# A gated recurrence on one core: Candidate's low-part product widened to 128 columns, so that it carries both parts of its input

## What is computed

```
z = sigmoid(xz_t + h @ U_z + vz)
r = sigmoid(xr_t + h @ U_r + vr)
hh = tanh(xh_t + (r * h) @ U + vh)
h = (1 - z) * h + z * hh          # for t = 0 .. 127
x = x + all h
```

## Time and profile before

| | |
|---|---|
| runs before | 1509.14 us median of 3 (1508.98 to 1510.17) |
| profiled execution | 1510.37 us, span 1508.5 us, mean TensorE clock 0.998 |
| TensorE busy | 1499.4 us, 99% |
| VectorE, ScalarE busy | 84%, 78% |
| the recurrence | from 551 us to the end |

### The profile page before, as it was taken

One profiled execution on the slowest core, in us unless ns is written; L12 is line 12 of the kernel. 1 busy time (PEld: TensorE's weight loads), 2 busy tenths in 40 slices (PEclk: granted clock), 3 DMA queues, 4 the chain that ended last, 5 costly groups with the idle time before them and its releaser, 6 DMA issues.

```text
span 1508.5 us, 54085 instructions
## 1 busy us (share of the span) xinstructions
PE 1499.4 (99%) x22906; PEld 1175.1 (78%) x22906; DVE 1260.1 (84%) x2548; ACT 1173.7 (78%) x2726; POOL 315.7 (21%) x332
## 2 busy tenths in 40 slices
PE   9999999999999999999999999999999999999998
PEld 6874444444444467779999999999999999999998
DVE  7999999999999887777878787778787887776677
ACT  7989999999999835667777777777777777777444
POOL 1100111111110014322222222222222222222222
PEclk9999999999999999999999999999999999999999
DMA  5155365565638978533333333333333333320000
GB/s 199 33 159 183 96 200 140 130 159 136 191 84 133 142 115 102 74 52 23 48 20 48 48 20 49 43 25 48 20 46 48 20 48 20 48 41 3 31 32 31
DMA packets 545106, 116.61 MB, mean 77 GB/s; under 512 B 520160, under 2 KB 527200, under 8 KB 536160
## 3 DMA queue, kind: packets, MB, share of 16 engines
q1 hardware_dynamic: 537424, 82.14, 31.4%
q0 software_dynamic: 7008, 30.41, 10.7%
q10 hardware_dynamic: 432, 0.59, 0.1%
HBM read 66.47 MB, written 33.55 MB: 66 GB/s over the span
## 4 chain that ended last, share of the span: by engine, by line
PE 99%; DMA 0%; DVE 0%; ACT 0%; issue 0%; DVEq 0%
PE ps L1552 33%; PE ps L1617 22%; PE ps L1654 20%; PE ps L1666 15%; PE ps L1638 6%; PE ps L1570 2%; DMA AR<-in_w1f 0%; PE ps L1519 0%; PE ps L1583 0%; DVE ST L1381 0%; ACT ST L942 0%; ACT W L619 0%; DVE RL L1438 0%; ACT XS L626 0%; DVE ST L1386 0%
## 5 line engine op out<-in xcount | busy, mean ns | idle before, releaser
L1552 PE MATMUL ps<-XH,WH 128*128 128x512 f16 x1872 | 404.7, 379 | 0.0
L1552 PEld LDWEIGHTS ps<-XH,WH 128*128 128x128 f16 x1872 | 182.9, 98 | 220.2 <-issue 0.3
L1654 PE MATMUL ps<-HL,U 128*128 128x64 f16 x6112 | 221.0, 193 | 1.9 <-DVE HL L1485 1.9
L1773 POOL TENSOR_TENSOR ST<-ST 128x256 f32<-128x256 f32 x126 | 114.5, 909 | 490.9 <-ACT ST L934 490.9
L1666 PE MATMUL ps<-HL,U 128*128 128x64 f16 x4064 | 214.3, 206 | 0.0
L1654 PEld LDWEIGHTS ps<-HL,U 128*128 128x128 f16 x6112 | 204.8, 98 | 8.0 <-issue 2.0
L1666 PEld LDWEIGHTS ps<-HL,U 128*128 128x128 f16 x4064 | 183.5, 98 | 0.0
L1654 PEld LDWEIGHTS ps<-RL,U 128*128 128x128 f16 x4064 | 135.1, 98 | 6.5 <-issue 1.2
L1654 PE MATMUL ps<-RL,U 128*128 128x64 f16 x4064 | 139.4, 193 | 0.3 <-issue 0.3
L902 ACT ACTIVATE ST<-ps,dn 128x128 f32<-128x128 f32 x252 | 78.4, 361 | 71.2 <-PE ps L1666 71.1
L949 ACT ACTIVATE HL<-ST 128x128 f16<-128x128 f32 x208 | 53.3, 302 | 80.3 <-DVE ST L1477 80.3
(11 more groups left out here) (213 smaller groups left out, 3113.0 us busy)
## 6 DMA issues: line engine op xcount, KB each, us to landing
x_scratch<-AR SPq DMA_DIRECT2D x16, 1024.0 KB, 5.3
AR<-in_x POOLq DMA_DIRECT2D x15, 1024.0 KB, 7.9
AR<-HB POOLq DMA_DIRECT2D x11, 1024.0 KB, 7.0
raw<-x_scratch SPq DMA_DIRECT2D x88, 128.0 KB, 4.2
out_y<-raw SPq DMA_DIRECT2D x11, 1024.0 KB, 4.0
raw<-in_x SPq DMA_DIRECT2D x10, 1024.0 KB, 7.3
ST<-in_x SPq DMA_DIRECT2D x5, 1024.0 KB, 7.4
out_y<-AR SPq DMA_DIRECT2D x4, 1024.0 KB, 4.4
```

The source lines that it names most:

```text
L1552: op = pe.matmul(ps[b][:, :], v[:, g, wp, k, e * P:(e + 1) * P], y[:, xp, k, :], start=n == 0, stop=n == 11)
L1654: pe.matmul(ps[b][:, col:col + B], U[:, g, half, k, e * P:(e + 1) * P], S[:, k, 0], start=opens, stop=False, skip_group_check=True)
L1773: pool.tensor_tensor(zc, zc, Hst[(t + 1) % 2], ALU.mult).then_inc(s_zch, 1)
```

## The change

Candidate becomes "summed" in steps 2 to 119. It is still held, and now also joint. Its first product loses the 16 matmuls of U's high half, and its second takes 128 columns, [high | low], instead of 64. The results stand in two sets of 64 columns per feature tile. So ScalarE's `put_x` writes x's part, with half the scale, into both sets (128x512 instead of 128x256, from a broadcast input). VectorE adds the two sets with one TENSOR_REDUCE per half (`add_pair`, 128x256 to 128x128), placed where `add_x` for Candidate stood in the steps that are not held. ScalarE's tanh then reads the sum from SBUF and waits for VectorE (`s_pc`) instead of for TensorE (`s_C`). Two more constants are made in step 0.

```diff
+SUMMED = (2,)
...
         def is_joint(t, g):
 
-            return g == 0 and not held(t, g)
+            return g == 0 and not held(t, g) or summed_pair(t, g)
...
+        def summed_pair(t, g):
+
+            return g in SUMMED and HELD_FROM <= t < HELD_TO
+
+        def by_dve(t, g):
+
+            return not held(t, g) or summed_pair(t, g)
...
-            return sum(not held(n, g) for n in range(1, t + 1))
+            return sum(by_dve(n, g) for n in range(1, t + 1))
...
+        def pairs(b):
+            return ps[b].rearrange("p (e s b) -> p e b s", e=2, b=B)[:, :, :, 0:2]
...
-                    act.wait_ge(s_ux1, 5)
+                    act.wait_ge(s_ux1, 7)
...
-                if t == T - 1 and g == 2:
-                    act.wait_ge(s_pc, 2 * sums_by_dve(t - 1, 2))
-                elif t == HELD_FROM:
-                    act.wait_ge(s_pr if g == 1 else s_pc, 2 * (t - 1))
+                if by_dve(t - 1, g):
+                    act.wait_ge(s_pr if g == 1 else s_pc, 2 * sums_by_dve(t - 1, g))
...
+                if summed_pair(t, g):
+                    both = PS[:, first * 512:(first + 2) * 512].rearrange("p (e s b) -> p e s b", e=KT, b=B)[:, :, 0:2]
+                    x = XP[j % 2][:, g, :, tt * B:(tt + 1) * B].unsqueeze(2).to_broadcast([P, KT, 2, B])
+                    act.activation(both, x, ACT.Copy, scale=uh[:, 3 + g:4 + g]).then_inc(s_put[g], 1)
+                    return
...
-                        if held(t, 2):
+                        if summed_pair(t, 2):
+                            act.wait_ge(s_pc, 2 * sums_by_dve(t, 2) - 1 + h)
+                            act.activation(two(hg, h), two(hg, h), ACT.Tanh, scale=dn[:, scale(5)]).then_inc(s_hh, 1)
+                        elif held(t, 2):
...
+            def add_pair(dst, banks, done, sums):
+
+                for h in range(2):
+                    dve.wait_ge(*sums[h])
+                    dve.tensor_reduce(two(dst, h), pairs(banks[h]), AX.X, ALU.add).then_inc(done, 1)
+
...
+                    for g in (1, 2):
+                        dve.tensor_scalar(uh[:, 3 + g:4 + g], up[:, scale(3 + g)], 0.5 * HS, None, ALU.mult).then_inc(s_ux1, 1)
...
+                if summed_pair(t, 2):
+                    add_pair(hg, C, s_pc, [(s_C, 2 * u + 1), (s_C, 2 * u + 2)])
                 for h in range(0 if held(t, 2) else 2):
...
             def recurrent_first(t, banks, g, S, s_hi):
                 joint = is_joint(t, g)
-                per = 2 * B if joint else B
+                per = 4 * B if summed_pair(t, g) else 2 * B if joint else B
...
             def recurrent_second(t, banks, g, S, s_done):
                 joint = is_joint(t, g)
-                per = 2 * B if joint else B
+                per = 4 * B if summed_pair(t, g) else 2 * B if joint else B
+                n = 2 * B if joint else B
...
-                        op = pe.matmul(ps[b][:, col:col + per], U[:, g, 0, k, e * P:(e + 1) * P],
+                        op = pe.matmul(ps[b][:, col:col + n], U[:, g, 0, k, e * P:(e + 1) * P],
```

More of the change, by code:

```diff
@@ L110, in build @@
         mx, ag, ee, er, up, dn = (sb(n, 15 + NCH) for n in ("mx", "ag", "ee", "er", "up", "dn"))
-        dx1, ux1, bound, dc, uh = sb("dx1", 3), sb("ux1", 3), sb("bound", 4), sb("dc", 3), sb("uh", 4)
+        dx1, ux1, bound, dc, uh = sb("dx1", 3), sb("ux1", 3), sb("bound", 4), sb("dc", 3), sb("uh", 6)
         dx = sb("dx", 3 * NCH)[:, :].rearrange("p (c g) -> p c g", g=3)
@@ L899, in _ @@
                     for h in range(2):
-                        if held(t, 1):
+                        if summed_pair(t, 1):
+                            act.wait_ge(s_pr, 2 * sums_by_dve(t, 1) - 1 + h)
+                            act.activation(two(rg, h), two(rg, h), ACT.Sigmoid, scale=dn[:, scale(4)]).then_inc(s_r, 1)
+                        elif held(t, 1):
                             act.wait_ge(s_R, 2 * u + h + 1)
@@ L1429, in _ @@
                     continue
+                if summed_pair(t, 1):
+                    add_pair(rg, R, s_pr, [(s_R, 2 * u + 1), (s_R, 2 * u + 2)])
                 for h in range(0 if held(t, 1) else 2):
```

## The result

The changed kernel takes 1540.68 us (median of 4 runs, 1538.89 to 1540.90) against 1509.19 us (median of 4, 1508.98 to 1510.17): ratio 1.0205, 95% interval 1.0193 to 1.0217. It is slower by 31.5 us. The forecast was 1535 with a range of 1527 to 1552, and slower at 0.92. The profiled execution took 1540.83 us, span 1539.0, at a mean TensorE clock of 0.998.

The account below looks back on a forecast made before the run. TensorE sets the pace by its own matmul starts. 21.9 + 0.9 - 0.5 + 4.0 = 26.3 us on the profiled 1510.37 gives 1536.7; the runs' median lies 1.2 lower, so 1535 us, range 1527 to 1552.

Parts of the forecast that it names:

- the trade itself: Candidate's matmuls on TensorE: 0.466 us removed, 0.428 added, net -0.038 us a step, -4.5 us in 118 steps.
- The working's aside: With the skill's 25 ns per 64-column matmul, the trade would lose about 0.09 us a step, the sum 15 us higher.
- The wait for the low part of r·h: Before Candidate's second product: a 0.254 us wait opens, 102 steps (10 to 111) grow 0.215 each, 21.9 us.
- Steps 8 and 9: The low-part wait already binds there, so the wider product costs 0.43 us each: 0.9 us.
- The tail: VectorE's two reduces before tanh, 0.45 us each, delay h; waits for h add 4.0 us in the sum.
- rival (a): Reduces dear or queueing badly, waits for h's parts the larger stall: 1560 us; chance 0.14.
- The wait of 0.2 us in every eighth step: Step 50's class, 13 steps: reduces queue behind L1177, R waits 0.2 us for h, 2.6 us in all.
- Steps 112 to 119: Low part of h arrives 0.7 to 0.8 us later, use 0.43 later; about 0.1 left, so no wait.
- ScalarE's longer put: x's part takes 0.22 us more ahead of R's sigmoid; L1381's idle 0.63 us takes it: nothing.
- The mis-sized term: Steps 8 to 16: heavier VectorE tails than in step 50's class, 1.4 us added.
- (b): Rival: the wait for the low part never opens, only -4.5 us stays: 1505 us; chance 0.05.
- (c): Rival: the wait opens only up to the gain, or saved TensorE time is larger: 1506 to 1512 us; chance 0.03.

Follow-up runs that it names:

- after_low_first: The changed kernel with VectorE's low part of r·h put ahead of z's two sums in steps 8 to 111: 1517.69 us, ratio 1.0052.
- chosen_low_first: Against the kernel before: low part of r·h first in steps 8 to 111, the change in only 74 steps: 1507.26 us, ratio 0.9986.
- only_products: The changed kernel without the reduces, tanh reading only the first set in PSUM: 1533.37 us, ratio 1.0162 to the kernel before.
- after_pad8: The changed kernel with 8 extra unread 64-column matmuls behind Candidate's first product in steps 10 to 111: 1540.07 us.
- only_reduces: The changed kernel with Candidate's products as before, all into the first set, keeping the reduces and tanh from SBUF: 1517.21 us, ratio 1.0052.

## Why the prediction was right, and where it was off

**TensorE is the pace, and the trade itself is nearly even.** Right. -0.038 us a step was named; the steps 2 to 7 gave -0.038, and every undisturbed step of after_low_first and chosen_low_first -0.040. 58 ns for two narrow matmuls and 56 for a wide one hold, not the 25 ns that the Trainium skill (TensorE: Matmul & The Clock Gate, "Back-to-back issue gap") gives for 64 columns. The working's aside that the sum would be 15 us higher with 25 ns is wrong, and nothing rests on it. Where the wait binds, a step grows by the removed time less the spare, plus the added time less the removed: the removed time drops out, and 0.428 - 0.212 = 0.216 us is left. With 25 ns only the added time would be larger there, by 0.07 us, which makes about 9 us in all (an estimate from the skill's figure).

**The wait for the low part of r·h.** Right in place, size and reason: 0.254 us were forecast, and the second product starts 0.721 us after the first against the 0.720 that it makes (0.466 + 0.254). only_products shows it without the reduces, after_pad8 that it is idle time, after_low_first that it hangs on the place of the low part behind z's sums. A step grew by 0.226 rather than 0.215. The 0.01 is in the second product: its 16 matmuls started 56.5 ns apart (0.848 us from first to last), not 55.9. That is 1 us in all. Steps 8 and 9 without the reduces are 0.85 us, forecast 0.86; that is luck in part, since they are 0.64 and 0.21 and not 0.43 each.

**The tail.** A reduce was put at 0.45 us and measured 0.42 (L1415 in the rows below); the strided reading of PSUM shows no price near the 0.75 us that was kept open, and rival (a) falls with that. The wait of 0.2 us in every eighth step came in the class that was named, at 0.22 us. Step 50 of the changed kernel:

```profile
949.97 1.65 DVE L1198 SCALAR_TENSOR_TENSOR AR<-AR,up 128x256 f16<-128x256 f32 x2
950.11 1.07 PE L1700 MATMUL ps<-RL,U 128*128 128x128 f16 x16
...
950.50 0.72 POOL L1807 TENSOR_TENSOR ST<-ST 128x256 f32<-128x256 f32 x1 [3.87 <-ACT ST L952]
...
951.55 0.74 DVE L1415 TENSOR_REDUCE ST<-ps 128x128 f32<-128x256 f32 x2
...
953.28 0.51 ACT L970 ACTIVATE HL<-ST 128x128 f16<-128x128 f32 x2 [0.56 <-DVE ST L1510]
...
953.74 0.95 PE L1687 MATMUL ps<-HL,U 128*128 128x64 f16 x27
```

Counted from the second product's start, the first half of h's high part comes 1.22 us later than before (3.48 against 2.26), where 1.27 were worked out. R's product starts 0.145 us behind it, the least distance in the trace, where 0.08 were allowed. The two misses nearly cancel.

only_reduces has just 0.05 of the wait. Its reduces start 0.60 us sooner, counted from the second product's start (0.83 against 1.43). Of this 0.21 is the second product starting right behind the low part, which the working had as "itself ends 0.21 later". The other 0.39 it had not: the two splits ahead of the reduces (L1198) take 1.26 us there and 1.65 here. Against the 0.43 by which the wider product puts off the use, that leaves the missing 0.17. Step 74 of the changed kernel, where the splits take 1.27 us, has no such wait: it grew by 0.23. The 0.39 goes with GpSimd, as the last section shows; no run was made to test it.

Steps 112 to 119 were called free, with 0.1 us of margin. Steps 113 to 118 grew by 0.04 instead of shrinking by 0.04: R's second product, which waits for h's low part, starts 1.02 us behind its first and not 0.93.

ScalarE's longer put was counted as nothing. In step 20 that holds (L1402 still waits 0.64 us for z's product), but not in steps 8 to 16, where the waits for r·h's high part make 1.1 us; only_products has next to none of them in sum.

**The mis-sized term** is "Steps 8 to 16 have heavier VectorE tails still: I add 1.4". It was the one figure not worked out from rows. With 0.9 for steps 8 and 9 and 0.215 in the seven others that made 3.8 us; it was 6.69, and only_products has 2.63 of it. The tail is then about 4.1 us there, three times the guess. The stretch makes 2.9 of the 3.8 us by which the sum of growths was short, 2.7 of them by this term. Its working would have been that of step 50, with L1201 (the weight splits) in the place of L1177. The two halves share some waits in this stretch (only_reduces alone has 5.7 us), so 4.1 is the tail's part on top of the products and not its cost alone.

**The remainder.** The 30.1 us of growth leave 0.4 of the 30.5 between the two spans. Step 127, whose products are the same in both kernels, takes 0.48 us longer from its first to its last product. TensorE had been idle for 1.9 us ahead of this step in both. The granted clock was 0.50 (the 1.2 GHz level) from 1499.2 to 1502.6 us in the kernel before and from 1530.7 to 1534.1 in the changed one. Before, that covers R's products, and z's could not have started ahead of ScalarE's put of x's part, which ended at 1501.4, so it cost little there. In the changed kernel it starts 1.3 us later, counted from the step's first product, and falls on z's products; from their start to Candidate's first it is 2.54 us against 1.84. So this rest is argued to come from where the slow stretch falls, and belongs to no term of the sum.

**Rivals.** (b), faster, needed the low part to come 0.25 us sooner. It came when it did, and after_low_first shows what an early low part gives: -0.04 us in most steps, but with 8 us of tail the kernel is still slower than the one before, so (b) as priced (1505) would not have come even then. (c) is refuted by the interval.

## What to carry over

Work that is taken out of a saturated engine's queue was also cover for the next wait in it. Before counting it as gain, take the distance from the operand's end to its use, less the distance at which the same wait binds elsewhere in the trace; only that much comes back. While the wait binds, a step grows by the time that was added behind it less that spare, whatever the removed work cost. And if the operand's producer stands behind something that waits for the same engine, look at its order: moving one subtraction ahead of two sums was worth 23 us after the change and nothing before it. Where a stretch has extra work on the engine that gets the new operations, work out its queue from rows as well; a flat allowance was three times too small.

## What was not expected of the hardware

Groups by line and shape of the changed kernel: count, busy us, mean ns of one, idle before.

```profile
L1415 DVE TENSOR_REDUCE ST<-ps 128x128 f32<-128x256 f32 x236 | 93.7, 419 | 9.0 <-PE ps L1700 5.8
L960 ACT ACTIVATE ST<-ST,dn 128x128 f32<-128x128 f32 x236 | 90.0, 401 | 77.0 <-DVE ST L1415 74.6
```

The same of the kernel before:

```profile
L942 ACT ACTIVATE ST<-ps,dn 128x128 f32<-128x128 f32 x238 | 73.9, 361 | 11.8 <-PE ps L1666 9.3
```

Tanh of 128x128 with a scale read per partition takes 401 ns from SBUF. The same operation from PSUM took 361 ns in the kernel before (L942), so reading the sum from SBUF made it 40 ns slower. The Trainium skill (VectorE: DVE Perf Modes, "The TRN2 errata") gives ScalarE 224 cycles plus the elements from SBUF and 172 from PSUM, 43 ns apart at 1.2 GHz. The trace agrees with the difference, 401 against 361, and not with the times, which would be 293 and 250 ns by it. An estimate from the two rows: it takes about 0.04 us of each step's slack on the way to h.

VectorE's second split in step 50 (L1198, 128x256 from SBUF) and GpSimd's L1807 (128x256 in SBUF) are in each other's way, and the one that starts first keeps its pace. The steps are those with t mod 8 = 2 from 18 to 98. The second split starts 0.59 to 0.60 us behind the first. In the changed kernel, step 74 aside, GpSimd's operation starts 0.53 to 0.54 us behind the first split's start and takes 0.73 us, and the second split takes 1.05 to 1.07 us. In step 74 GpSimd starts 0.70 us behind it, when the second split is already running; there the split takes 0.68 us and GpSimd 1.10. In only_reduces and after_low_first GpSimd starts 0.63 to 0.82 us behind, and the split takes 0.66 to 0.68 us and GpSimd 0.98 to 1.18. What the two share is not shown by these runs, and the profile's times of GpSimd are rough. A shift of 0.1 us in when one engine starts thus moved the reduces by 0.4 us.
